# A fused layer pair of 33 pipelined steps on one core: centering split around the variances, one scatter moved ahead on GpSimd, one register load moved ahead on TensorE

## The chip, the core and the metric

The kernel runs on one core of one Trainium2 chip. The metric is the device time in microseconds (us) of one execution. Engines are named as the profile names them: PE is TensorE (PEld its weight loads, PEldq the sequencer that feeds them), DVE is VectorE, ACT is ScalarE, POOL is GpSimd, SP is SyncE (which only starts transfers here).

## The reference, cut to what matters

The input holds 128 sequences of 64 tokens with 256 features. Two layers follow each other; each picks its weights by a number that belongs to the sequence.

```python
def layer0(x, condition, ...):          # condition 0, 1, 2 per sequence
    out_nr  = gelu(x @ w1_nr  + b1_nr)  @ w2_nr  + b2_nr      # condition 0
    out_tsr = gelu(x @ w1_tsr + b1_tsr) @ w2_tsr + b2_tsr     # condition 1
    h = gelu(x @ w1_sr + b1_sr)                               # condition 2: 256 -> 512
    h = gelu(h @ w2_sr + b2_sr)                               # 512 -> 256
    out_sr = h @ w3_sr + b3_sr
    y = x + where(condition == 0, out_nr, where(condition == 1, out_tsr, out_sr))
    return layernorm(y) * gamma + beta

def layer1(x, domain_id, ...):          # 16 experts, 64 wide
    hidden = gelu(x @ down_W.T + down_b)
    hidden = hidden @ expert_W[idx].T + expert_b[idx] + domain_emb[idx]
    y = x + hidden @ up_W.T + up_b
    return layernorm(y) * ln_gamma + ln_beta
```

The whole reference computes all three branches and selects; the kernel computes only the branch that a sequence needs.

## The kernel before, in words

**Slots and steps.** The kernel sorts the sequences by condition on the chip and packs four of one kind into a slot of 256 tokens, held as two tiles of 128 tokens. Here there are 33 slots: first those of the three-layer kind (`sr`, slots 0 to 8), then those of the two-layer kinds. A software pipeline handles one slot per step. In step g, TensorE finishes the first layer of slot g (`ps_z`), transposes the normalised slot g-1 (`ps_t`), runs the adapter of slot g-2 (`ps_u`, `ps_d`) and begins slot g+1 (`ps_h`). VectorE works on the statistics of slot g and, later in the same step, on those of the second norm of slot g-2, splits the input of slot g+2 into a high and a low part, and finishes slot g-3. Fp32 products are made from three products of high and low parts, so the low parts `x_lo` (VectorE, L665) and `h_lo` (GpSimd, L482) are operands of TensorE.

**What sets the order.** The order on every engine is written by hand. Each engine runs its own loop over the steps: two steps per turn on VectorE, ScalarE, GpSimd and SyncE, four steps per turn on TensorE (L281 is the jump back). Engines wait for each other by counting semaphores, named for what is ready: `h1_lo`, `x_lo`, `rstd`, `zn_act`, `yt_act`.

**TensorE, two-layer step** (`finish_other`): the slot's kind is loaded into a register (`kind_of`), `down` makes `ps_d` (L1222), a branch picks the kind of step, `last_layer` makes `ps_z` (L1157 with the high parts, L1162 with the low ones; their addresses are worked out from the kind in registers), `start_two` makes `ps_h` (L1089), then `adapter` loads the expert's two table addresses (`tables_of`), transposes (L1179), adds residuals (L1124) and multiplies with the tables (L1209).

**TensorE, three-layer step** (`finish_sr`): kind, `down`, first half of the middle layer (L1260, L1261, and L1263 with `h_lo`), first half of the next slot's first layer (L1089, which waits for `x_lo`), second half of the middle layer (its L1263 waits for `h1_lo`), input residual (L1124), second half of the first layer, the table addresses, transposes, `last_layer`, the expert.

**VectorE** (L828 to L856): `first_stats` (`st<-ps_z`, L691), `first_moments` (`mv`, L698), `variances` (`ve`, L703), `center` (`n`, two tiles, L727), `second_stats` (`st<-ps_u`, L714), `input_low` (`x_lo`, L665), `second_moments` (L721), `minus_mean` (`nm`, L707), `finish` (`o`, L767), `add_bias` (L677), `copy_second_tables` (L743). `nm` lets ScalarE write `zn`.

**GpSimd**: in a three-layer step it makes the low part of `h2`, of the first half of `h1` (`h0_lo`), the powers `rs` of the variances (L489), the low part of the second half of `h1` (`h1_lo`), and then starts two indirect DMAs, the scatters of tile 1 (L508) and tile 0 (L515) of a slot finished a step earlier. The scatters begin with step 4. In a two-layer step the low parts are half as large, in the same order.

## Time and profile before

| | |
|---|---|
| median of 3 timed runs | 267.99 us (267.77 to 269.57) |
| time of the profiled execution | 270.54 us |
| its span, first to last instruction | 268.7 us |
| PE busy | 249.6 us (93%) |
| DVE busy | 206.6 us (77%) |
| ACT busy | 190.9 us (71%) |
| POOL busy | 174.8 us (65%) |
| mean granted TensorE clock | 0.987 |
| register loads by TensorE's sequencer (L338) | 66 |

The page gives busy times per engine and the chain of work that ended last. TensorE is nearly always busy, but the end of a matmul is modelled in this profile, so what counts is where its idle times stand and what ended them. Between about 60 and 105 us the steps are three-layer ones, 11.3 us each; from about 118 to 240 us they are two-layer ones, four of them in 23.6 us.

### The profile page before, as it was taken

How to read it: one execution, taken by the hardware profiler on the slowest of the kernel's cores; microseconds unless marked ns; L12 is line 12 of the kernel's file. 1: busy time of each engine (PE TensorE's matmuls, PEld its weight loads, DVE VectorE, ACT ScalarE, POOL GpSimd, SP SyncE). 2: the span in 40 equal slices, each digit the busy share in tenths (PEclk: the TensorE clock that was granted, in tenths of full speed). 3: DMA queues.
4: the chain of work that ended last, by engine and by line, in shares of the span. 5: the costliest groups of instructions: out<-in, count | busy, mean ns of one | idle time of the engine just before them, and what ended most of it. 6: DMA issues, size and time to landing. Idle time of an engine off the chain costs nothing.

```text
span 268.7 us, 8023 instructions
## 1 busy us (share of the span) xinstructions
PE 249.6 (93%) x2114; PEld 219.9 (82%) x2115; DVE 206.6 (77%) x717; ACT 190.9 (71%) x450; POOL 174.8 (65%) x188
## 2 busy tenths in 40 slices
PE   8998999989898898899999999999999999999960
PEld 7698898979788797799988888998888899887630
DVE  6769643472835628599989989998998999899893
ACT  3578479577494777578688877868887887878640
POOL 3134474463755857588778878887887888779451
PEclk9999999999999999999999999999999999999995
DMA  6472011011121120223323333332333333231315
GB/s 182 105 260 63 12 42 43 4 43 30 32 61 41 39 68 29 59 68 96 90 83 93 88 91 84 88 98 78 98 88 88 82 94 98 78 99 54 74 42 121
DMA packets 41640, 20.71 MB, mean 77 GB/s; under 512 B 37431, under 2 KB 39181, under 8 KB 41614
## 3 DMA queue, kind: packets, MB, share of 16 engines
q1 hardware_dynamic: 37625, 12.10, 18.7%
q0 software_dynamic: 2592, 7.08, 7.5%
q10 hardware_dynamic: 1396, 1.19, 1.7%
q8 instruction: 15, 0.25, 0.4%
q14 instruction: 12, 0.09, 0.1%
HBM read 11.69 MB, written 8.65 MB: 76 GB/s over the span
## 4 chain that ended last, share of the span: by engine, by line
PE 64%; DVE 13%; issue 9%; POOL 6%; ACT 4%; DVEq 1%; ACTq 1%; DMA 1%; POOLq 0%
PE ps_h L1089 20%; PE ps_z L1157 11%; PE ps_u L1209 6%; PE ps_z L1162 5%; PE ps_z L1124 4%; PE ps_t L1179 4%; PE ps_d L1222 4%; POOL h_lo L482 3%; PE ps_u L1124 3%; POOL rs L489 2%; DVE x_lo L665 2%; DVE st L714 2%; DVE n L727 2%; ACT yt L937 2%; ACT h L903 1%
## 5 line engine op out<-in xcount | busy, mean ns | idle before, releaser
L482 POOL TENSOR_TENSOR h_lo<-h,h_hi 128x256 fp32r<-128x256 f32 (+1 forms) x75 | 70.4, 939 | 51.3 <-ACT h L903 50.1
L910 ACT ACTIVATE zn<-ps_z,nm,rs 128x256 f32<-128x256 f32 x66 | 33.7, 561 | 30.5 <-DVE nm L707 28.9
L691 DVE BATCH_NORM_STATS2 st<-ps_z 128x6 f32<-128x256 f32 x66 | 24.8, 416 | 37.1 <-PE ps_z L1162 37.0
L489 POOL TENSOR_TENSOR rs<-ve,minus_half 128x4 f32<-128x4 f32 (+1 forms) x38 | 38.2, 1005 | 19.8 <-DVE ve L703 19.2
L903 ACT ACTIVATE h_hi<-ps_h,per_feature_sb 128x256 fp32r<-128x256 f32 x84 | 38.6, 493 | 13.9 <-PE ps_h L1089 8.9
L903 ACT ACTIVATE h<-ps_h,per_feature_sb 128x256 f32<-128x256 f32 x84 | 38.8, 499 | 0.0
L508 POOL DMA_INDIRECT out<-o,out_rows_now x27 | 34.9, 1292 | 4.8 <-issue 4.8
L937 ACT ACTIVATE yt<-ps_t,per_feature_sb 128x256 f32<-128x256 f32 x66 | 34.0, 574 | 4.2 <-PE ps_t L1179 3.4
L665 DVE TENSOR_TENSOR x_lo<-x,x_hi 128x512 fp32r<-128x512 f32 x33 | 31.2, 946 | 6.3 <-ACT x_hi L889 6.3
L1209 PE MATMUL ps_u<-tables,stack 65*64 x132 | 35.6, 392 | 0.3 <-ACT stack L921 0.3
L1209 PE MATMUL ps_u<-second_table,stack 65*64 65x256 f32 x132 | 35.6, 392 | 0.0
L1157 PE MATMUL ps_z<-last_hi,h_hi 128*128 (+1 forms) x132 | 35.5, 304 | 0.0
L1157 PE MATMUL ps_z<-last_lo,h_hi 128*128 (+1 forms) x132 | 32.1, 279 | 0.0
L515 POOL DMA_INDIRECT out<-o,out_rows_now x27 | 26.5, 980 | 8.2 <-issue 8.2
L767 DVE SCALAR_TENSOR_TENSOR o<-n,rs,per_feature_sb 128x256 f32<-128x256 f32 x64 | 28.8, 490 | 0.3
L727 DVE SCALAR_TENSOR_TENSOR n<-ps_u,mv,per_feature_sb 128x256 f32<-128x256 f32 x66 | 28.8, 477 | 0.0
L1157 PEld LDWEIGHTS ps_z<-last_hi,h_hi 128*128 128x128 f32 x132 | 24.8, 188 | 4.1 <-issue 4.1
L1089 PE MATMUL ps_h<-x_hi,w_two_hi 128*128 128x256 f32 x96 | 27.4, 285 | 0.0
L714 DVE BATCH_NORM_STATS2 st<-ps_u 128x6 f32<-128x256 f32 x66 | 25.1, 421 | 2.3 <-PE ps_u L1209 1.0
L1089 PE MATMUL ps_h<-x_hi,w_two_lo 128*128 128x256 f32 x96 | 26.8, 279 | 0.0
L1089 PE MATMUL ps_h<-x_lo,w_two_hi 128*128 128x256 f32 x96 | 26.7, 278 | 0.0
L921 ACT ACTIVATE stack<-ps_d,per_feature_sb 64x128 f32<-64x128 f32 x66 | 24.4, 369 | 1.9 <-PE ps_d L1222 0.7
(150 smaller groups left out, 649.4 us busy)
## 6 DMA issues: line engine op xcount, KB each, us to landing
x<-in_x_feat SPq DMA_DIRECT2D x130, 64.0 KB
out<-o SPq DMA_DIRECT2D x18, 64.0 KB, 2.0
out<-o,out_rows_now POOLq DMA_INDIRECT x54
last_sb<-in_last_w SPq DMA_DIRECT2D x1, 768.0 KB, 4.8
w_sr_sb<-in_w_sr SPq DMA_DIRECT2D x1, 512.0 KB, 3.9
w_sr_sb<-in_w_sr ACTq DMA_DIRECT2D x1, 512.0 KB, 4.8
w_two_sb<-in_w_two SPq DMA_DIRECT2D x1, 512.0 KB, 5.6
out<-o ACTq DMA_DIRECT2D x6, 64.0 KB, 2.4
```

Source lines behind the costliest of these rows:

```text
L482: pool.tensor_tensor(dst, full, high.bitcast(F32), ALU.subtract).then_inc(ready, 1)
L489: pool.tensor_tensor(RS[p][:, norms, :], VE[p][:, norms, :], half_of_two[:, norms, :], ALU.pow).then_inc(rstd, 1)
L508: pool.indirect_dma_start(out_rows, row, O[p][:, 1, :], None).then_inc(sc_out[p], 16)
L665: dve.tensor_tensor(XL[p][:, :, :, :], XF[p][:, :, :, :], XH[p][:, :, :, :].bitcast(F32), ALU.subtract).then_inc(x_lo, 1)
L714: dve.bn_stats(ST[1][p][:, t, :], UP[p][:, t, :]).then_inc(stat[1], 1)
L727: ins = dve.scalar_tensor_tensor(out=N2[p][:, t, :], in0=UP[p][:, t, :], scalar=MV[step][:, 1, t, 0:1], in1=G2[:, 0, :], op0=ALU.subtract, ...
L903: ins = act.activation(dst[:, m, :], src[m], ACT.Gelu, bias=COL[:, bass.ds(col + m, 1)])
L910: ins = act.activation(ZN[:, t, :], ZP[p][:, t, :], ACT.Identity, bias=NM[p][:, t:t + 1], scale=RS[p][:, 0, t:t + 1])
L937: ins = act.activation(YT[q][:, c, :], TP[:, c, :], ACT.Identity, bias=COL[:, COL_BETA1 + c:COL_BETA1 + c + 1], scale=COL[:, COL_G1 + c:CO ...
L1089: ins = pe.matmul(out_ap, lhs[a], rhs[b], start=first and n == 0, stop=last and n == 2)
L1157: pe.matmul(ZP[p][:, t, :], h2h[:, c, t * P:(t + 1) * P], rows(half, c), start=False, stop=False)
L1209: ins = pe.matmul(UP[p][own, t, :], S[p][:, t, own], table, start=False, stop=(t == TT - 1))
```

## The change: what it does

It has three parts. On VectorE, `center` is cut into its two tiles: tile 0 now stands between `first_stats` and `first_moments`, tile 1 stays behind `variances`. On GpSimd, tile 1's scatter moves ahead of the low part of h1's second half in the three-layer branch; in the two-layer branch it stays behind both low parts. On TensorE, `tables_of` moves from the middle of the step to its start, behind `kind_of` and ahead of `down`.

GpSimd, in its loop over the steps:

```diff
                 with pool.If(g + 1 < b_sr):
                     low(h1l[:, 0:2, :], h1[:, 0:2, :], h1h[:, 0:2, :], h0_full, h0_lo, g + 1)
                     powers(g, i, p, where)
+                    if where in (MAIN, LAST2):
+                        store_tile1(g - 4, p)
                     low(h1l[:, 2:4, :], h1[:, 2:4, :], h1h[:, 2:4, :], h1_full, h1_lo, g + 1)
                 with pool.Else():
...
-                store(g, where)
+                    if where in (MAIN, LAST2):
+                        store_tile1(g - 4, p)
+                if where in (MAIN, LAST2):
+                    store_tile0(g - 4, p)
```

VectorE:

```diff
+            def center_tile(slot, p, step, t):
+
                 dve.wait_ge(stat[1], 2 * TT * slot + 2 * TT)
-                for t in range(TT):
-                    ins = dve.scalar_tensor_tensor(out=N2[p][:, t, :], in0=UP[p][:, t, :],
-                                                   scalar=MV[step][:, 1, t, 0:1], in1=G2[:, 0, :],
-                                                   op0=ALU.subtract, op1=ALU.mult)
-                ins.then_inc(n2_made, 1)
+                return dve.scalar_tensor_tensor(out=N2[p][:, t, :], in0=UP[p][:, t, :],
+                                                scalar=MV[step][:, 1, t, 0:1], in1=G2[:, 0, :],
+                                                op0=ALU.subtract, op1=ALU.mult)
...
                 for slot in on_slot(g, 0, where):
                     first_stats(slot, p)
+                for slot in on_slot(g, 3, where):
+                    center_tile(slot, q, p, 0)
                 for slot in on_slot(g, 0, where):
                     first_moments(slot, p)
                 variances(p, BOTH)
                 for slot in on_slot(g, 3, where):
-                    center(slot, q, p)
+                    center_tile(slot, q, p, 1).then_inc(n2_made, 1)
```

TensorE:

```diff
-            def adapter(g, p, where):
-
-                at = [tables_of(slot) for slot in on_slot(g, 2, where)]
+            def adapter(g, p, where, at):
+
...
-                at = [tables_of(slot) for slot in on_slot(g, 2, where)]
                 pe.wait_ge(h2_full, g + 1)
...
+                at = None
                 if where != DRAIN and (where != HEAD or g >= 0):
                     kind = kind_of(pe, g)
+                    for slot in on_slot(g, 2, where):
+                        at = tables_of(slot)
                 for slot in on_slot(g, 2, MAIN if where == DRAIN else where):
                     down(slot, p, MAIN)
```

The order of GpSimd in the three-layer branch of a loop step, before (names in brackets are the semaphores it waits for):

```order
L481 REGISTER_ALU
L482 TENSOR_TENSOR h_lo<-h,h_hi 128x512 [waits h0_full]
L489 TENSOR_TENSOR rs<-ve,minus_half 128x4 [waits var]
L482 TENSOR_TENSOR h_lo<-h,h_hi 128x512 [waits h1_full]
L550 UNCONDITIONAL_BRANCH
```

and now:

```order
L481 REGISTER_ALU
L482 TENSOR_TENSOR h_lo<-h,h_hi 128x512 [waits h0_full]
L489 TENSOR_TENSOR rs<-ve,minus_half 128x4 [waits var]
L505 REGISTER_ALU
L508 DMA out<-o,out_rows_now 8960x256 [waits o1_made]
L482 TENSOR_TENSOR h_lo<-h,h_hi 128x512 [waits h1_full]
L544 UNCONDITIONAL_BRANCH
```

Tile 1's scatter stands between the powers and the second low part; before, it came behind the branch.

TensorE at the start of a step in its loop, before (`ps_d` is `down`, L1157 the first products of `last_layer`):

```order
L338 ISA
L338 TENSOR_LOAD ids
L1222 MATMUL ps_d<-yt,per_feature_sb 64x128 [waits yt_act]
L1222 MATMUL ps_d<-yt,per_feature_sb 64x128 x3
L1342 COMPARE_AND_BRANCH
L1303 REGISTER_ALU
L1157 ISA [waits h1_hi]
L1157 MATMUL ps_z<-last_hi,h_hi 128x256
```

and now (all lines behind the edits are numbered four or five higher, L1157 is L1161):

```order
L338 ISA
L338 TENSOR_LOAD ids
L338 ISA
L338 TENSOR_LOAD ids
L1226 MATMUL ps_d<-yt,per_feature_sb 64x128 [waits yt_act]
L1226 MATMUL ps_d<-yt,per_feature_sb 64x128 x3
L1347 COMPARE_AND_BRANCH
L1305 REGISTER_ALU
L1161 ISA [waits h1_hi]
L1161 MATMUL ps_z<-last_hi,h_hi 128x256
```

The second load stood between L1089 and the transposes of L1179 and is gone there.

VectorE at the start of a step in its loop, before:

```order
L691 BN_STATS st<-ps_z 128x6
L695 ISA
L698 BN_AGGR mv<-st 128x2 [waits stat1]
L698 BN_AGGR mv<-st 128x2
L699 REGISTER_ALU
L703 TENSOR_SCALAR ve<-mv 128x4 [waits stat1]
L725 REGISTER_ALU
L727 SCALAR_TENSOR_TENSOR n<-ps_u,mv,per_feature_sb 128x256 [waits stat2]
L727 SCALAR_TENSOR_TENSOR n<-ps_u,mv,per_feature_sb 128x256
L714 BN_STATS st<-ps_u 128x6 [waits u_ps]
```

and now:

```order
L690 BN_STATS st<-ps_z 128x6
L729 REGISTER_ALU
L730 SCALAR_TENSOR_TENSOR n<-ps_u,mv,per_feature_sb 128x256 [waits stat2]
L694 ISA
L697 BN_AGGR mv<-st 128x2 [waits stat1]
L697 BN_AGGR mv<-st 128x2
L698 REGISTER_ALU
L702 TENSOR_SCALAR ve<-mv 128x4 [waits stat1]
L730 SCALAR_TENSOR_TENSOR n<-ps_u,mv,per_feature_sb 128x256 [waits stat2]
L713 BN_STATS st<-ps_u 128x6 [waits u_ps]
```

One of the two centering instructions now stands ahead of the moments and of `ve`.

## Rows read from the trace of the kernel before

**Rows 1.** From the page: share of the chain that ended last, by engine

```profile
PE 64%; DVE 13%; issue 9%; POOL 6%; ACT 4%; DVEq 1%; ACTq 1%; DMA 1%; POOLq 0%
```

**Rows 2.** Timeline of TensorE, steps of three-layer slots (start us, us, line, tiles, idle before)

```profile
59.85 0.38 PE L1089 MATMUL ps_h<-x_hi,w_sr_hi 128*128 128x256 f32 x1 [0.91 <-DVE x_lo L665]
80.80 0.63 PE L1263 MATMUL ps_t<-h_lo,w_sr_hi 128*128 128x256 f32 x4
82.32 0.39 PE L1089 MATMUL ps_h<-x_hi,w_sr_hi 128*128 128x256 f32 x1 [0.89 <-DVE x_lo L665]
93.59 0.39 PE L1089 MATMUL ps_h<-x_hi,w_sr_hi 128*128 128x256 f32 x1 [0.89 <-DVE x_lo L665]
```

**Rows 3.** Timeline of VectorE in one of these steps

```profile
77.97 0.76 DVE L691 BATCH_NORM_STATS2 st<-ps_z 128x6 f32<-128x256 f32 x2 [4.96 <-PE ps_z L1162]
78.87 0.25 DVE L698 BATCH_NORM_AGGREGATE mv<-st 128x2 f32<-128x6 f32 x2
79.16 0.17 DVE L703 TENSOR_SCALAR ve<-mv 128x4 f32<-128x4 f32 x1
79.25 0.88 DVE L727 SCALAR_TENSOR_TENSOR n<-ps_u,mv,per_feature_sb 128x256 f32<-128x256 f32 x2
80.72 1.55 DVE L665 TENSOR_TENSOR x_lo<-x,x_hi 128x512 fp32r<-128x512 f32 x1
```

**Rows 4.** Timeline of GpSimd in the same step

```profile
79.41 1.04 POOL L489 TENSOR_TENSOR rs<-ve,minus_half 128x4 f32<-128x4 f32 x1 [0.83 <-DVE ve L703]
80.44 1.27 POOL L482 TENSOR_TENSOR h_lo<-h,h_hi 128x512 fp32r<-128x512 f32 x1
```

**Rows 5.** Timeline, one slot earlier than the first scatter: VectorE, then GpSimd

```profile
58.28 1.52 DVE L665 TENSOR_TENSOR x_lo<-x,x_hi 128x512 fp32r<-128x512 f32 x1
57.97 1.28 POOL L482 TENSOR_TENSOR h_lo<-h,h_hi 128x512 fp32r<-128x512 f32 x1
```

**Rows 6.** Timelines around the last three-layer step: GpSimd, then TensorE

```profile
102.97 1.28 POOL L482 TENSOR_TENSOR h_lo<-h,h_hi 128x512 fp32r<-128x512 f32 x1
104.75 0.63 PE L1263 MATMUL ps_t<-h_lo,w_sr_hi 128*128 128x256 f32 x4
106.46 0.66 PE L1124 MATMUL ps_z<-ident,x 128*128 128x128 f32 x4 [1.08 <-DVE x L677]
```

**Rows 7.** Timelines in a two-layer step: GpSimd, GpSimd, VectorE

```profile
130.42 0.72 POOL L482 TENSOR_TENSOR h_lo<-h,h_hi 128x256 fp32r<-128x256 f32 x1
131.32 1.29 POOL L508 DMA_INDIRECT out<-o,out_rows_now  x1 [0.18 <-issue]
130.92 0.77 DVE L665 TENSOR_TENSOR x_lo<-x,x_hi 128x512 fp32r<-128x512 f32 x1
```

**Rows 8.** Register loads of TensorE's sequencer (PEldq), duration ns min/median/max, start us

```profile
L338 PEldq TENSOR_LOAD <-ids x1: 309/309/309, 123.3 to 123.3; - x1
L338 PEldq TENSOR_LOAD <-ids x1: 545/545/545, 120.7 to 120.7; - x1
L1144 PEldq EVENT_SEMAPHORE  x1: 51/51/51, 121.7 to 121.7; - x1
```

**Rows 9.** Line 1157 behind a loop's jump, then in another step, same columns

```profile
L1157 PEldq ALU_OP  x1: 32/32/32, 124.7 to 124.7; - x1
L1157 PEld LDWEIGHTS ps_z<-last_hi,h_hi x1: 186/186/186, 124.8 to 124.8; 128*128 128x128 f32 x1
L1157 PEldq ALU_OP  x1: 32/32/32, 130.1 to 130.1; - x1
L1157 PEld LDWEIGHTS ps_z<-last_hi,h_hi x1: 187/187/187, 130.6 to 130.6; 128*128 128x128 f32 x1
```

**Rows 10.** The jump back of TensorE's loop from 85 us on, same columns

```profile
L281 PEldq FUSED_REGOPS  x6: 78/78/78, 89.3 to 217.5; - x6
```

**Rows 11.** Timelines: ScalarE's wait for TensorE, then TensorE's for ScalarE

```profile
134.32 0.47 ACT L903 ACTIVATE h_hi<-ps_h,per_feature_sb 128x256 fp32r<-128x256 f32 x1 [1.37 <-PE ps_h L1089]
136.13 0.66 PE L1222 MATMUL ps_d<-yt,per_feature_sb 128*64 128x128 f32 x8 [0.24 <-ACT yt L937]
```

More of the change, by code:

```diff
@@ L515, in store_tile0 @@
                 pool.indirect_dma_start(out_rows, row, O[p][:, 0, :], None).then_inc(sc_out[p], 16)
-            def store(g, where):
-                if where in (MAIN, LAST2):
-                    store_tile1(g - 4, p)
-                    store_tile0(g - 4, p)
             def scale(slot, q, p, count):
@@ L723, in center @@
             def center(slot, p, step):
+                center_tile(slot, p, step, 0)
+                center_tile(slot, p, step, 1).then_inc(n2_made, 1)
+            def center_tile(slot, p, step, t):
                 dve.wait_ge(stat[1], 2 * TT * slot + 2 * TT)
-                for t in range(TT):
-                    ins = dve.scalar_tensor_tensor(out=N2[p][:, t, :], in0=UP[p][:, t, :],
-                                                   scalar=MV[step][:, 1, t, 0:1], in1=G2[:, 0, :],
-                                                   op0=ALU.subtract, op1=ALU.mult)
-                ins.then_inc(n2_made, 1)
+                return dve.scalar_tensor_tensor(out=N2[p][:, t, :], in0=UP[p][:, t, :],
+                                                scalar=MV[step][:, 1, t, 0:1], in1=G2[:, 0, :],
+                                                op0=ALU.subtract, op1=ALU.mult)
             def last_variances(slot, p, q):
@@ L1232, in adapter @@
                 for slot in on_slot(g, 2, where):
-                    expert(slot, p, where, at[0])
+                    expert(slot, p, where, at)
             def start_sr(g, q, where, half):
@@ L1271, in middle_layer_half, with finish_sr @@
                 return middle_layer(g, half, False)
-            def finish_sr(g, p, where):
+            def finish_sr(g, p, where, at):
                 q = 1 - p
@@ L1295, in finish_sr, with finish_other @@
                 for slot in on_slot(g, 2, where):
-                    expert(slot, p, where, at[0])
-            def finish_other(g, p, where, kind):
+                    expert(slot, p, where, at)
+            def finish_other(g, p, where, kind, at):
                 for slot in on_slot(g, 0, where):
@@ L1304, in finish_other @@
                 start_two(g, 1 - p, where)
-                adapter(g, p, where)
+                adapter(g, p, where, at)
             kind = None
@@ L1342, in _ @@
                     with pe.If(g >= b_sr):
-                        finish_other(g, p, where, kind)
+                        finish_other(g, p, where, kind, at)
                     with pe.Else():
-                        finish_sr(g, p, where)
+                        finish_sr(g, p, where, at)
                 if where == HEAD and g < 0:
```

## The prediction, on record before the changed kernel ran

> **What bounds the kernel now.** I read the chain of waits first, then TensorE's timeline for what ended its idle times, then the other engines' timelines at those places. TensorE holds 64% of the chain, and VectorE and GpSimd together 19% [rows 1]. So a wait is worth something where TensorE stands still. The reader is to see two regimes. In three-layer steps TensorE stops once per step ahead of L1089, for 0.89 to 0.91 us, until `x_lo` is there [rows 2]; 59.85, 82.32 and 93.59 are shown, and the fourth such wait is at 71.06 with 0.85. In two-layer steps it hardly waits for data; there its own sequencer is the thing to look at [rows 8, 9].
>
> **Why `x_lo` is late.** In the step of rows 3 and 4, `x_lo` starts at 80.72 and takes 1.55 us, while GpSimd's second `h_lo` runs from 80.44 to 81.71 [rows 3, 4]. In a two-layer step `x_lo` takes 0.77 us, and it ends 0.55 us after GpSimd's `h_lo` ends (131.69 against 131.14), although the scatter runs from 131.32 on [rows 7]. In the three-layer step the distance is the same: 82.27 against 81.71 is 0.56. So `x_lo` stands still until GpSimd's subtraction is over, needs some 0.6 us then, and a scatter that starts after it does not hold it up. The Trainium skill, page "SBUF — State Buffer", section "SBUF: two separate sides", states the same as an exclusive lock: a VectorE operation with two SBUF inputs and a GpSimd operation that reads SBUF don't share, the one that starts first keeps the ports, the other blocks fully. The trace agrees on the blocking (0.55 and 0.56 us behind GpSimd's end). [...]
>
> **Part 1, the scatter ahead of the second `h_lo`** (four steps, g = 4 to 7). `rs` ends at 80.45 [rows 4]; the scatter takes 1.29 us and starts 0.18 after what is ahead of it [rows 7], so `h_lo` starts at about 80.45 + 0.18 + 1.29 = 81.9 and not 80.44. `x_lo` then has the ports to itself and is ready at about 80.7 + 0.65 = 81.35. TensorE's L1263 group starts at 80.80 and ends at 81.43 as modelled [rows 2], so the wait goes. That is 0.85 + 0.89 + 0.89 = 2.6 us for the waits at 71.06, 82.32 and 93.59. The delayed `h_lo` ends at about 83.2 plus what part 2 adds, 0.2; TensorE would ask for it 2.5 us after L1089 begins (two groups of matmuls later), at about 83.9. It is covered by 0.5 us. In the last three-layer step no first layer lies between the two halves: TensorE asks at 104.75, the `h_lo` of 102.97 to 104.25 will end 1.67 later, at 105.9, and TensorE waits 1.2 us [rows 6]. Today it waits 1.08 us right behind it for the input's bias, which `x_lo` would have brought forward [rows 6]; the one wait takes the place of the other, and I charge 0.2 us. The second scatter is no longer behind the first without a break, but nobody waits for it.
>
> **Part 2, centering.** It removes and adds no instruction. `mv` starts at 78.87, 0.14 after the statistics end [rows 3]; one tile of `n` is half of 0.88, and fills that gap. So `ve` comes 0.44 - 0.14 = 0.3 later at most, and 0.2 if the tile overlaps its neighbours as the two tiles overlap; I take 0.2. `x_lo` starts 0.14 to 0.2 earlier. In the step before the first scatter this changes who comes first: `x_lo` starts at 58.28 and `h_lo` at 57.97 [rows 5]; now `x_lo` at about 58.1 and `h_lo`, which follows `rs` and so `ve`, at 57.97 + 0.2 = 58.17. If VectorE is first, the wait of 0.91 at 59.85 goes too; if not, it grows by 0.2. I take the gain, as the likelier by some 0.07 us. In two-layer steps `x_lo` ends 0.55 behind GpSimd's `h_lo` [rows 7], which follows `ve` where `rs` waits for it; nothing is gained there, and `zn` can come 0.2 later. I charge nothing for that: TensorE reaches its transposes behind twelve matmuls of L1089, and if this cover is gone a step pays up to 0.2. At the drain the powers stand on the chain and the last ordinary step pays 0.2.
>
> **Part 3, the register load.** TensorE's sequencer loads the kind in 0.309 us and the two table addresses in 0.545 [rows 8]. Where the second load stands now, the matmuls of L1089 cover it, and behind it the sequencer waits for `zn` anyway (the wait of L1144 at 121.7, 0.4 after the load ended at 121.3) [rows 8]; its removal there gives TensorE nothing. At the start of a step the sequencer works out the addresses of L1157 after the load. Behind the loop's jump it finishes at 124.7, and the first weights go at 124.8: no slack. In another step it finishes at 130.1 and they go at 130.6: 0.4 of slack [rows 9]. A second load of 0.545, with its address operation, is some 0.55 us more. It is paid in full behind the jump, and mostly covered elsewhere, since a late step leaves `zn` early for the next one. The loop jumps back six times from 89 us on, once among the three-layer steps [rows 10]: 5 x 0.55 = 2.75 us. At the sixth, `down` would be some 0.35 late and takes that from what the wait at 93.59 gives back. Bounds: 0 if the load can be overlapped; 22 two-layer steps x 0.545 = 12 us if no slack counted; the row at 124.7 is the nearest, hence 2.75.
>
> **The sum.** -0.91 - 2.63 + 0.2 + 0.35 = -3.0 for the three-layer steps, + 2.75 for the two-layer ones, + 0.2 at the drain: -0.05 us on the profiled time of 270.54 (span 268.7), which is 2.55 above the median of 267.99. The steps are the same in both, so I subtract from the median: 267.9 us, no change. A measurement of this kernel can tell about 1%, or 2.7 us, from no change.
>
> **Rivals.**
> 1. *Faster: the load isn't paid.* If the second load comes while the sequencer is held anyway (at 136.13 `down` waits for `yt` [rows 11]), or costs 0.1, the three-layer gain stands alone: 267.99 - 3.0 + 0.2 = 265.2. Connected with it: ScalarE gets TensorE's signal 1.37 us late once in four steps [rows 11], in a step in which the loads of several sequencers fall together; if moving TensorE's load ends this, each of five is worth 0.24 (TensorE's own wait) to 1.37, so 1.2 to 6.9 us more. With the middle of the lower half of it, some 2, and the load unpaid, 263.5. For: in a step such as that of rows 11 the sequencer has idle time in plenty. Against: rows 9 leave no slack. Chance 0.30 in all.
> 2. *Slower: every two-layer step pays.* The slack of 0.4 in an ordinary step is smaller than 0.55. If `zn` is not early enough for the sequencer to catch up, each of the 17 steps that are not behind a jump pays 0.15 to 0.2. That is 3 us: 267.9 + 3.0 = 270.9, slower by 1.1%. The point from which it decides is 0.4 us of added sequencer time in a step whose `zn` is not earlier than now. Chance 0.13.
> 3. *Slower: the scatter holds the ports.* By the mechanism of rows 7 a GpSimd operation that is first blocks `x_lo`. If the scatter were first in the three-layer steps (it starts at about 80.8, `x_lo` at 80.55) and blocked as a subtraction does, `x_lo` would end at 80.8 + 1.29 + 0.55 = 82.6, and the waits would grow by 0.35 and not shrink: 267.9 + 2.6 + 1.0 = 271.5. [...] Against: rows 7 show a scatter beside `x_lo` with no delay. Chance 0.07.
> 4. *The forecast*, gains and costs that cancel: 0.50, with 266.3 to 269.8 as its own range (the race for the ports is 1.1 us, each load may be 0.1 us off, which is 0.5).
>
> **How the numbers follow.** Faster by over 1% (below 265.3): most of rival 1 and the lower edge of the forecast, 0.29. Slower by over 1% (above 270.7): rivals 2 and 3 and a little of the forecast, 0.18. Within 1%: 0.53. The range that leaves out no more than 2 in 10 runs from 264.2, inside rival 1, to 270.9, the time of rival 2.
>
> **What would show it.** The waits for `x_lo` ahead of L1089 at some 70, 81 and 91 us should be under 0.2 us, `x_lo` near 0.7 us there; one new wait for `h_lo` of about 1 us in the last three-layer step. The load of the tables should stand 0.1 behind that of the kind, and L1157 should begin 0.5 us later after `down` only behind the jump, making four two-layer steps 24.1 us and not 23.6. If they still take 23.6, part 3 is wrong and rival 1 holds; if `x_lo` still takes 1.5 us, part 1 is wrong.

## The result and the profile after

The changed kernel takes 270.49 us (median of 11 runs, 269.17 to 272.02), the kernel before 268.96 us (11 runs, 267.54 to 271.26). The ratio is 1.0072, 95% interval [1.0045, 1.0098]: slower by 0.7%, where I forecast 267.9 us and no change. The time lies in the forecast's range, but the likeliest case was not what happened.

The two profiled executions show nothing of it: both have a span of 268.7 us (270.53 us after, 270.54 before), at a clock of 0.988 and 0.987. So the first question is what the profile of before stood for; the second, where the parts went.

**Three-layer steps.** VectorE, then GpSimd, of the changed kernel, in the step that answers to [rows 3, 4]:

```profile
77.78 0.48 DVE L730 SCALAR_TENSOR_TENSOR n<-ps_u,mv,per_feature_sb 128x256 f32<-128x256 f32 x1
78.85 0.68 DVE L664 TENSOR_TENSOR x_lo<-x,x_hi 128x512 fp32r<-128x512 f32 x1
79.60 0.13 DVE L706 SCALAR_TENSOR_TENSOR nm<-mv,rs 128x2 f32<-128x2 f32 x1
79.71 2.75 DVE L769 SCALAR_TENSOR_TENSOR o<-n,rs,per_feature_sb 128x256 f32<-128x256 f32 x2
82.38 0.34 DVE L676 TENSOR_SCALAR x<-x,slot_bias 128x256 f32<-128x256 f32 x1
```

```profile
77.95 1.04 POOL L489 TENSOR_TENSOR rs<-ve,minus_half 128x4 f32<-128x4 f32 x1 [1.62 <-DVE ve L702]
79.20 1.24 POOL L508 DMA_INDIRECT out<-o,out_rows_now  x1 [0.20 <-issue]
80.47 1.30 POOL L482 TENSOR_TENSOR h_lo<-h,h_hi 128x512 fp32r<-128x512 f32 x1
```

`x_lo` takes 0.68 us and not 1.55, as forecast, and TensorE no longer waits for it. But the two tiles of `o` take 2.75 us where they took 0.87: the first alone takes 2.35 us and not 0.47, and ends only 0.3 us behind the second `h_lo`, which is over at 81.77. The bias of the input behind them (L676) is late, and TensorE waits for that:

```profile
83.07 0.66 PE L1128 MATMUL ps_z<-ident,x 128*128 128x128 f32 x4 [0.40 <-DVE x L676]
```

The waits of TensorE's matmuls, summed over the changed kernel (line waited for: us in total, times, longest), have lost "DVE x_lo", 3.5 us in 4 waits before. Of the rows below the first stood at 1.1 us in one wait before, and the third is new:

```profile
PE ps_z L1128 <- DVE x L676: 1.8, 4, 0.5
PE ps_d L1226 <- ACT yt L941: 1.1, 5, 0.3
PE ps_t L1266 <- POOL h_lo L482: 1.0, 1, 1.0
```

**Two-layer steps.** The two loads now stand together behind the jump (TensorE's sequencer, duration ns min/median/max, first and last start us):

```profile
L338 PEldq TENSOR_LOAD <-ids x2: 308/426/543, 145.5 to 146.0; - x2
```

and `down` comes late six times:

```profile
PEld ps_d L1226 <- issue: 2.9, 6, 0.6
```

The wait of ScalarE of [rows 11] is there once in each turn of the loop (four steps), in the profile of before as in that of after (here the second of five in the changed kernel). I call a wait of 1.3 us and more for `ps_h` a late signal:

```profile
156.76 0.47 ACT L907 ACTIVATE h_hi<-ps_h,per_feature_sb 128x256 fp32r<-128x256 f32 x1 [1.42 <-PE ps_h L1093]
```

**A table of all profiles.** From TensorE's timelines: T1 is the start of the first last layer (L1157 before, L1161 after) behind the three-layer steps, T2 that of the one 21 steps later. "Late" counts the late signals from 117 us on.

```
kernel                           T1      T2 - T1   late   time us   ratio to before
before, first profile            119.08  123.99    5      270.54    (this execution)
before, profiled again (e9)      119.06  121.66    1      268.20    (this execution)
after                            117.33  125.75    5      270.49    1.0072
e1  load only                    119.14  123.49    3      269.99    1.0052
e2  scatter + split centering    117.39  122.57    1      267.57    0.9975
e3  scatter only                 117.48  121.50    1      266.69    0.9963
e4  split centering only         114.79  122.57    1      264.86    0.9866
e5  split + load                 114.98  126.25    5      268.74    1.0020
e6  x_lo issued earlier          114.61  135.95    0      279.42    1.0420
e7  e2, bias ahead of o          115.07  128.43    0      271.14    1.0111
e8  e5 once more                 115.84  126.49    5      268.98    1.0020
e10 e5, four loads at the top    120.14  134.93    8      282.91    1.0562
e11 e5, tile 0 not stored        115.93  121.57    0      264.13    0.9859
e12 e4, tile 0 not stored        114.81  121.61    0      264.13    0.9867
e13 after, tile 0 not stored     117.18  121.61    0      266.19    0.9935
e14 e5, second scatter later     115.77  132.90    0      277.28    1.0360
e15 split in three-layer only    114.78  121.43    1      263.46    0.9837
```

The rest of the document reads this table. The scatter and the centering show mostly in T1, the load in T2 - T1. T1 also holds the start of the kernel: the first last layer of all stands at 53.7 us in most profiles, but 0.8 to 0.9 us later in e8 and e11, 0.4 in e14 and e15, and 1.7 in e10.

### The profile page after: what moved, and what is told of

Its sections match the earlier page's. It is cut to its first block, busy times and chain, and to the rows that moved or that the text cites. A ratio compares the mean times of both kernels' runs of the same rounds, so it can differ in the third digit from the quotient of the medians.

```text
span 268.7 us, 8050 instructions
## 1 busy us (share of the span) xinstructions
PE 251.2 (93%) x2114; PEld 219.9 (82%) x2115; DVE 209.4 (78%) x717; ACT 192.1 (71%) x450; POOL 175.5 (65%) x188
## 4 chain that ended last, share of the span: by engine, by line
PE 64%; issue 11%; DVE 11%; POOL 6%; ACT 4%; DVEq 2%; ACTq 0%; POOLq 0%
PE ps_h L1093 18%; PE ps_z L1161 11%; PE ps_u L1213 7%; PE ps_z L1166 5%; PE ps_z L1128 4%; PE ps_d L1226 4%; PE ps_t L1183 4%; POOL h_lo L482 3%; PE ps_u L1128 3%; POOL rs L489 2%; DVE o L769 2%; DVE st L713 2%; PE ps_t L1038 2%; ACT yt L941 2%; DVE st L690 1%
## 5 line engine op out<-in xcount | busy, mean ns | idle before, releaser
L482 POOL TENSOR_TENSOR h_lo<-h,h_hi 128x256 fp32r<-128x256 f32 (+1 forms) x75 | 71.4, 953 | 47.5 <-ACT h L907 46.0
L489 POOL TENSOR_TENSOR rs<-ve,minus_half 128x4 f32<-128x4 f32 (+1 forms) x38 | 38.2, 1006 | 23.5 <-DVE ve L702 23.2
L769 DVE SCALAR_TENSOR_TENSOR o<-n,rs,per_feature_sb 128x256 f32<-128x256 f32 x64 | 36.5, 609 | 0.3
L1161 PE MATMUL ps_z<-last_hi,h_hi 128*128 (+1 forms) x132 | 35.5, 304 | 0.0
L664 DVE TENSOR_TENSOR x_lo<-x,x_hi 128x512 fp32r<-128x512 f32 x33 | 28.5, 863 | 6.0 <-ACT x_hi L893 6.0
L1161 PE MATMUL ps_z<-last_lo,h_hi 128*128 (+1 forms) x132 | 32.2, 279 | 0.0
L730 DVE SCALAR_TENSOR_TENSOR n<-ps_u,mv,per_feature_sb 128x256 f32<-128x256 f32 x66 | 30.6, 470 | 0.0
L1161 PEld LDWEIGHTS ps_z<-last_hi,h_hi 128*128 128x128 f32 x132 | 24.8, 188 | 4.1 <-issue 4.1
```

Source lines behind the costliest of these rows:

```text
L482: pool.tensor_tensor(dst, full, high.bitcast(F32), ALU.subtract).then_inc(ready, 1)
L489: pool.tensor_tensor(RS[p][:, norms, :], VE[p][:, norms, :], half_of_two[:, norms, :], ALU.pow).then_inc(rstd, 1)
L730: return dve.scalar_tensor_tensor(out=N2[p][:, t, :], in0=UP[p][:, t, :], scalar=MV[step][:, 1, t, 0:1], in1=G2[:, 0, :], op0=ALU.subtract ...
L769: dve.scalar_tensor_tensor(out=O[o][:, t, :], in0=N2[q][:, t, :], scalar=RS[p][:, 1, t:t + 1], in1=G2[:, 1, :], op0=ALU.mult, op1=ALU.add) ...
L1161: pe.matmul(ZP[p][:, t, :], h2h[:, c, t * P:(t + 1) * P], rows(half, c), start=False, stop=False)
```

## The experiments

**e9: the kernel before, unchanged, once more.**

> The kernel before, unchanged, profiled once more: how much of its first profile is one outcome among several. Theory J (the kernel before has executions with a late signal of TensorE in each turn of the loop and executions without): this one shows between 0 and 4 waits of ScalarE of over 1.3 us for `ps_h` in the two-layer steps and not 5, and a span shorter by 0.4 to 0.5 us for each that is missing (264.5 to 268.3 us). Rival K (they belong to this order of instructions): again five, and a span within 0.4 us of 268.7.

One wait of over 1.3 us (168.97, 1.44), a span of 266.4 us, 268.2 us in all. T1 is the same to 0.02 us, T2 - T1 is 2.33 us shorter: 0.58 us for each of four late signals. So theory J holds, with 0.58 and not 0.4 to 0.5 us for each. The wait, ScalarE of e9:

```profile
168.97 0.47 ACT L903 ACTIVATE h_hi<-ps_h,per_feature_sb 128x256 fp32r<-128x256 f32 x1 [1.44 <-PE ps_h L1089]
```

The profile that the prediction was made from was one of the longer outcomes of this kernel: that explains most of the 1.6 to 2.6 us by which it stood above the medians, and why two profiles of one span can belong to kernels 0.7% apart.

**e1: the register load alone.** Part 3's lines of the diff on the kernel before.

```diff
                     kind = kind_of(pe, g)
+                    for slot in on_slot(g, 2, where):
+                        at = tables_of(slot)
```

> Only part 3: TensorE loads the two table addresses with the kind, ahead of `down`; scatter and centering stay as before. Theory A (the load behind the loop's jump is paid on TensorE's path): 5 two-layer jumps x 0.4 to 0.55 us and one three-layer jump x 0.35, so +2.0 to +3.1 us, a ratio of 1.008 to 1.012, with about six waits put down to issue ahead of `down` (L1226 of the kernel after), 0.4 to 0.5 us each. Rival B (the loss of the whole comes from the split centering, whose `ve` is later in the two-layer steps): ratio 1.000, within 0.002. Rival C (every two-layer step pays 0.15 to 0.2 us beside the jumps): +5 us, ratio 1.02.

1.0052 [1.0018, 1.0086], +1.4 us. Seven waits of `down` for issue, 3.0 us in all, as theory A says, but only +1.83 in T2 - T1 against e9, with three late signals and not one. A price below A's. The turns of the loop without a late signal tell the two apart: they take 23.27 and 23.22 us here (119.14 to 142.41, 213.64 to 236.86), and 22.99 and 22.96 in e9 (119.06 to 142.05, 188.81 to 211.77); the step of the jump takes 6.00 and 5.95, and in e9 5.71 and 5.69. So on the kernel before, the load itself costs some 0.3 us behind the jump in these two turns, about half of the 0.55 of the prediction.

**e2: scatter and split centering, without the load.** `at = [tables_of(slot) ...]` stands again where it stood before, in `adapter` and `finish_sr`.

> Parts 1 and 2 without part 3: the addresses are loaded where the kernel before loads them. Theory A: what the three-layer steps gained in the profile (1.75 us up to the first two-layer step, with a jump of 0.35 in it) stands alone, -1.8 to -2.1 us, a ratio of 0.992 to 0.994, and the waits ahead of `down` put down to issue are gone. Rival B (the split centering costs 0.1 to 0.2 us in each of 22 two-layer steps): a ratio of 1.000 to 1.008, with two-layer steps still longer than in the kernel before.

0.9975 [0.9945, 1.0006]; 2.9 us below the changed kernel by the medians, 2.6 by the two ratios. That is what the load costs this kernel; four late signals come with it.

**e3: the scatter alone.** GpSimd's lines of the diff on the kernel before.

```diff
                     powers(g, i, p, where)
+                    if where in (MAIN, LAST2):
+                        store_tile1(g - 4, p)
                     low(h1l[:, 2:4, :], h1[:, 2:4, :], h1h[:, 2:4, :], h1_full, h1_lo, g + 1)
```

> Part 1 alone: tile 1's scatter ahead of the second `h_lo` on GpSimd; centering and load as before. Theory A: the waits for `x_lo` at three of the four places go (0.85, 0.89, 0.89), but `o` on VectorE, which reads two SBUF operands, is now held for about 1.9 us by the scatter and the `h_lo` behind it, and the bias of the input comes 0.4 to 0.5 us too late for TensorE in each of them: -2.63 + 4 x 0.45 = -0.8 us, ratio 0.997; the wait of 0.91 for `x_lo` at 59.85 stays. Rival D (a scatter does not hold `o`; the late `o` is an effect of the split centering): `o` stays near 0.87 us for both tiles, and the gain is 2.4 us, ratio 0.991.

0.9963 [0.9931, 0.9996]. The time is theory A's, the reason only half. Here it is `nm` that is held and not `o`. VectorE, then GpSimd, of e3:

```profile
80.04 0.68 DVE L664 TENSOR_TENSOR x_lo<-x,x_hi 128x512 fp32r<-128x512 f32 x1
80.78 1.59 DVE L706 SCALAR_TENSOR_TENSOR nm<-mv,rs 128x2 f32<-128x2 f32 x1
82.37 0.87 DVE L766 SCALAR_TENSOR_TENSOR o<-n,rs,per_feature_sb 128x256 f32<-128x256 f32 x2
```

```profile
79.97 1.04 POOL L508 DMA_INDIRECT out<-o,out_rows_now  x1 [0.20 <-issue]
81.04 1.31 POOL L482 TENSOR_TENSOR h_lo<-h,h_hi 128x512 fp32r<-128x512 f32 x1
```

`nm` (0.12 us when free) begins 0.26 us ahead of `h_lo` and still ends with it, at 82.37. It was held from 80.78 on, while of GpSimd's operations only the scatter ran.

**e4: the split centering alone.** VectorE's lines of the diff on the kernel before.

```diff
+                for slot in on_slot(g, 3, where):
+                    center_tile(slot, q, p, 0)
                 for slot in on_slot(g, 0, where):
                     first_moments(slot, p)
                 variances(p, BOTH)
                 for slot in on_slot(g, 3, where):
-                    center(slot, q, p)
+                    center_tile(slot, q, p, 1).then_inc(n2_made, 1)
```

> Part 2 alone: centering divided around the variances. Theory A: the race for the ports at the step without a scatter goes to VectorE (-0.9 us); the other three-layer steps keep their wait for `x_lo`, perhaps shorter by 0.1; two-layer steps cost nothing or 0.1 us each: between -0.9 and +1.3 us, ratio 0.997 to 1.005. Rival B (the split is what made the whole slower): +2 to +4 us, ratio 1.008 to 1.015, two-layer steps longer by 0.1 to 0.2 us each, with the statistics or `rs` later by as much.

0.9866 [0.9818, 0.9913], 264.86 us: far outside what both theories gave. T1 is 4.3 us earlier. VectorE, then GpSimd, of e4:

```profile
78.26 0.68 DVE L665 TENSOR_TENSOR x_lo<-x,x_hi 128x512 fp32r<-128x512 f32 x1
79.01 1.10 DVE L707 SCALAR_TENSOR_TENSOR nm<-mv,rs 128x2 f32<-128x2 f32 x1
80.10 0.87 DVE L770 SCALAR_TENSOR_TENSOR o<-n,rs,per_feature_sb 128x256 f32<-128x256 f32 x2
```

```profile
78.40 1.69 POOL L482 TENSOR_TENSOR h_lo<-h,h_hi 128x512 fp32r<-128x512 f32 x1
```

The split wins the race in every three-layer step, not in one: `x_lo` begins 0.14 us ahead of `h_lo` where it began 0.28 behind [rows 3, 4], a shift of 0.42. GpSimd's subtraction is held instead (1.69), and `nm` is held until that is over at 80.1, but nothing longer; the scatter comes later and `o` runs beside it in 0.87. Steps take 10.1 us, against 11.26 before and 10.67 with the scatter ahead. So the scatter, which I priced at -2.6 us, costs 2.7 us once the centering is split (e2 against e4: 267.57 and 264.86; T1 117.39 and 114.79).

**e6: another way to win the race.** On the kernel before:

```diff
                 for slot in on_slot(g, -2, where):
                     input_low(slot, p)
+                for slot in on_slot(g, 2, where):
+                    second_stats(slot, p)
```

(and `second_stats` gone from ahead of it).

> The kernel before, with one edit only: `x_lo` is issued on VectorE ahead of the statistics of `ps_u` and not behind them, so it starts some 0.7 us earlier; centering is not split. Theory F (the gain of the split centering is that VectorE's `x_lo` comes ahead of GpSimd's second `h_lo`): `x_lo` takes 0.7 us, the waits for it ahead of TensorE's first layer go, three-layer steps take 10.1 to 10.3 us and not 11.26, the time is 264.5 to 266 us, ratio 0.984 to 0.990. Rival G (the gain comes from something else in the split, the tile of `n` that is done early or the later `ve`): the steps stay above 10.6 us and the ratio above 0.993.

T1 is 114.61: steps of 10.1 us are there without any split, so theory F holds for the mechanism. The time is 279.42 us, 1.042 [1.0385, 1.0454], far above F's range, since two-layer steps now take 6.2 to 6.8 us: VectorE stands waiting for `x_hi`, and the statistics behind it are late. Theory F had left that out.

```profile
147.78 0.82 DVE L665 TENSOR_TENSOR x_lo<-x,x_hi 128x512 fp32r<-128x512 f32 x1 [0.85 <-ACT x_hi L889]
148.53 0.75 DVE L714 BATCH_NORM_STATS2 st<-ps_u 128x6 f32<-128x256 f32 x2
```

**e7: the bias ahead of `o`.** On e2:

```diff
+                for slot in on_slot(g, -2, where):
+                    dve.wait_ge(x_lo, slot + 1)
+                    add_bias(slot, p)
                 for slot in on_slot(g, 3, where):
                     finish(slot, i - 2 if p == 0 else i - 1, q, where)
```

(and `add_bias` gone from behind it).

> Parts 1 and 2 without part 3 (267.57 us), with one further edit: VectorE adds the input's bias ahead of the two tiles of `o`, not behind them. Theory H (what part 1 costs is that `o` stands still from the middle of the scatter to the end of the second `h_lo`, and delays the bias TensorE waits for): the waits of 0.4 to 0.5 us for `x` go and three-layer steps fall from 10.66 to 10.1 to 10.3 us, 265.0 to 266.2 us. Rival I (the cost of part 1 is the second `h_lo` itself, which comes later for the middle layer, or the bias is held up as `o` is): steps stay at 10.5 to 10.7 us and the time within 0.7 us of 267.6.

The waits for `x` are gone, T1 is 115.07 and the steps take 10.1 us, as theory H says. But the bias itself is now what stands still, as rival I had it:

```profile
79.12 2.60 DVE L676 TENSOR_SCALAR x<-x,slot_bias 128x256 f32<-128x256 f32 x2
81.65 0.15 DVE L767 COPY out_rows_now<-out_rows 128x2 int32 x1
81.72 0.87 DVE L769 SCALAR_TENSOR_TENSOR o<-n,rs,per_feature_sb 128x256 f32<-128x256 f32 x2
```

It ends at 81.7 and not at 83.0, which is enough for TensorE. In two-layer steps the new order costs 5.9 us in T2 - T1 (most steps take 6.0 to 6.3 us), and the kernel takes 271.14 us, 1.0111 [1.0076, 1.0145], outside both theories' ranges. The cause of that cost stays open.

**e5, e8: the load on the split centering.** Part 3's lines on e4; e8 with a second `tables_of(slot)` ahead of the first.

> The split centering together with the moved register load, without the moved scatter. The split alone ran at 264.86 us, its four two-layer steps at 23.2 us with no signal of TensorE's later than 1.3 us in them after the first. Theory A (the load is paid in TensorE's sequencer behind the loop's jump, 0.35 to 0.5 us at each of six jumps): +2.1 to +3.0 us, 267.0 to 267.9 us, and 23.6 to 23.7 us for every four two-layer steps also where ScalarE gets no late signal. Rival E (the load costs 0.2 us per jump or less, and the rest is that `h_hi` on ScalarE waits 1.3 to 1.6 us for TensorE's `ps_h` more often): +0.5 to +1.2 us where such waits stay at one, +0.45 more for each further one, and 23.3 to 23.4 us for four steps without one.

> The split centering and the moved load, with the load of the two addresses issued twice at the top of each step of TensorE (the first one's values unused): twice the suspected cost. Theory A (no slack behind the jump, 0.4 us in an ordinary step): another 0.55 us behind each of six jumps and 0.1 to 0.2 in each of the 17 other two-layer steps: +5 to +7 us over the kernel with one load. Rival E (most of a load is covered also behind the jump): less than +2.5 us over it.

268.74 and 268.98 us, both 1.0020 ([0.9998, 1.0041] and [0.9997, 1.0044]). e8's unused load was dropped in compiling, so it is a second run of e5 and its expectation was not put to a test. The load costs 3.9 us here, more than either theory said. Of it, 0.3 us lie in the one three-layer step behind a jump (84.1 to 94.5: 10.41 us, 10.13 in e4). Four two-layer steps take 24.0 us, each turn with one late signal of 1.40 to 1.62 us. Without the load they take 23.2, with a late signal only in the first two-layer step.

**e11, e12: the same pair without the second scatter.** In both, GpSimd doesn't store tile 0 (the count that waits for scatters is halved to match):

```diff
-                row = bass.IndirectOffsetOnAxis(ap=OUT_NOW[p][:, 0:1], axis=0)
-                pool.indirect_dma_start(out_rows, row, O[p][:, 0, :], None).then_inc(sc_out[p], 16)
```

> The split centering and the moved load; GpSimd does not store tile 0 (its scatter, the second of a step, is left out). Theory M (TensorE's signals are held when a group of first-layer matmuls ends beside the second scatter, which the later `down` brings about): no wait of ScalarE over 1.3 us for `ps_h` in the two-layer steps, four of them at 23.6 us and not 24.0, 1.8 to 2.2 us less than with the second scatter, 266.5 to 267 us. Rival N (the late signals have nothing to do with the scatter): again four or five of them, four steps at 24.0 us, 268.2 to 268.8 us.

> The split centering alone, with tile 0 not stored (the second scatter of a step is left out): the pair to the kernel with the load moved and the same left out. With both theories 264.0 to 264.9 us, four two-layer steps at 23.2 us or less, since no signal was late in the kernel with both scatters after its first two-layer step. The difference of the pair is then the load's own price: 0.4 us at each of six jumps, 2.0 to 2.8 us, under theory A; under 1 us if the sequencer's time is covered.

Both 264.13 us (0.9859 and 0.9867, each within 0.0027): the pair shows no difference. No signal is late. `down` still waits for the sequencer eight times, 3.4 us in all:

```profile
PEld ps_d L1225 <- issue: 3.4, 8, 0.5
```

and the step of the jump takes 6.02 us (138.90 to 144.92), but the four up to 162.11 take 23.21, as in e12: the steps behind it take 5.7 us where e12's take 5.8, so TensorE makes up for it. So theory A falls for the kernels with the split centering: in their two-layer steps the load itself costs nothing that can be seen, and nearly all of its 3.9 us in e5 go by way of the late signals. The one three-layer step behind a jump does pay (10.39 us against 10.12), and on the kernel before, where free steps average 5.74 us (e9), e1's jumps pay 0.3. Theory M holds, and more strongly than I had put it (264.1 and not 266.5). One reservation: leaving out the scatter also frees GpSimd for some 1.3 us in each step, and no run takes away the late signals alone.

**e13: the changed kernel without the second scatter.**

> The changed kernel with tile 0 not stored (the second scatter of a step is left out). Theory M (the moved load costs only through TensorE's signals that are held beside the second scatter): no wait of ScalarE over 1.3 us for `ps_h` in the two-layer steps, four of them at 23.2 us; the changed kernel's 270.5 us less five turns of the loop x 0.8 us, 266.2 to 267.0 us. Rival A (the load is paid by TensorE's sequencer, 0.4 us at each of six jumps, in the changed kernel): 268.5 to 269.5 us.

266.19 us, 0.9935 [0.9910, 0.9960], no late signal, T2 - T1 121.61. Leaving the scatter out brings e4 0.7 us, and the changed kernel 4.3. The remaining 3.6 are what the load costs by way of the late signals, by these medians; e2 gives 2.9. A turn of the loop with a late signal is 0.8 us longer here (24.0 against 23.2 us).

**e10: a truly longer top of the step.** On e5, both halves of the last layer take their own load of the kind, and each tile its own load of the addresses:

```diff
-                    kind = kind_of(pe, g)
+                    kind = (kind_of(pe, g), kind_of(pe, g))
-                        at = tables_of(slot)
+                        at = [tables_of(slot)[0], tables_of(slot)[1]]
```

> The split centering and the moved load, with the step's top made longer for TensorE's sequencer: the kind and the addresses come in four loads of one value (0.31 us each, and what goes with them) and not in one of one value and one of two (0.31 + 0.545), some 0.4 to 0.5 us more in each step. (The kernel that was to load twice had lost its unused load in compiling: its trace counts 68 loads by TensorE, as the one with one load does, so it was a second run of that kernel.) Theory A (what the sequencer does at the top is paid behind the loop's jump): another 0.4 to 0.5 at each of six jumps, and 0 to 0.2 in each of 17 other two-layer steps, +2.4 to +6 us over 268.74. Rival L (once TensorE is behind the scatters, the size of the load doesn't matter): within 1 us of 268.7.

The trace counts 132 loads by TensorE and not 68: a step loads twice 0.31 and twice 0.54 us, so some 0.9 us were added and not 0.4 to 0.5. 282.91 us, 1.0562 [1.0531, 1.0594]. `down` waits for its sequencer ("issue") in 19 steps:

```profile
PEld ps_d L1228 <- issue: 19.1, 19, 1.5
```

T2 - T1 grows by 8.7 us over e5, 0.41 in each of 21 steps. Eight signals are late and not five, so a part of it goes by way of them. Rival L falls. The first 0.55 us at the top were covered (e11), the next 0.9 cost less than a half of their length. That is the mechanism of the prediction's rival 2, beyond a point that the change had not reached.

**e14: the second scatter later.** On e5, GpSimd fills an unused tile ahead of it and waits for that to be done.

```diff
+                pool.memset(idle[:, :], 0.0).then_inc(idle_made, 1)
+                pool.wait_ge(idle_made, slot + 1)
```

> The split centering and the moved load (268.74 us), nothing left out; GpSimd fills an unused tile of 128x256 ahead of the second scatter, so that it starts an estimated 0.3 to 0.6 us later. Theory M with the moment deciding (a signal is held where the group of matmuls ends when the second scatter has begun or is about to; the groups ended from 0.09 before... after its start to 0.19 us ahead of it): all groups now end 0.3 us or more ahead of it, no wait over 1.3 us in the two-layer steps, four of them at 23.2 to 23.3 us, 264.6 to 265.6 us. Rival O (the scatter's descriptors are the cause wherever it stands, or GpSimd's added work is paid): late signals again, or steps over 5.9 us, and 268.5 us or more.

277.28 us, 1.0360 [1.0316, 1.0405]. No wait of 1.3 us, as theory M says (every group ends 1.06 us or more ahead of the scatter), but the edit was too large to decide what that is worth: GpSimd, of e14,

```profile
150.26 0.33 POOL L514 MEMSET idle<- 128x256 f32 x1
151.43 0.96 POOL L519 DMA_INDIRECT out<-o,out_rows_now  x1 [0.84 <-POOL idle L514]
```

starts the second scatter 1.18 us behind the end of the first, where e5 starts it 0.30 behind, and `h_lo` is late for TensorE's weight loads (8.5 us in 22 waits; 2.9 in 4 in e5). Whether a small delay would save the load is open.

**e15: split only where a three-layer step follows.** On e4, `with dve.If(g + 1 < b_sr):` around the split order and `dve.Else()` around the old one.

> Centering is split only in steps that are followed by a three-layer step, by a branch on VectorE; in the others both tiles of `n` stand behind the variances as in the kernel before; scatter and load as in the kernel before. Theory P (the split costs 0.02 to 0.03 us in each two-layer step and gains only in three-layer ones): three-layer steps at 10.1 us, the whole from 264.2 to 264.9 us. Rival Q (the branch, or signals of TensorE held more often in the rhythm of the old order, cost more than that): 265.2 to 266.5 us, with one or more additional waits of over 1.3 us for `ps_h`.

263.46 us, 0.9837 [0.9808, 0.9865], below theory P's range; T2 - T1 is 121.43, 1.14 less than in e4. T1 is as in e4 though all began 0.4 us later: the step into T1, which now has the old order, takes 6.84 us and not 7.16. It is the fastest of all kernels here, 2.3% below the changed kernel by the two ratios. Both profiles have one late signal, so the split costs 0.05 us in each of 21 two-layer steps, and the branch nothing that can be seen.

## Why the prediction was wrong

Against the kernel before as e9 shows it, the changed one gains 1.7 us up to T1 and loses 4.1 from T1 to T2. I had -3.0 (with the jump in it) and +2.75, so both terms were off, in the same direction. That the sum of -0.05 us met the two profiled times to 0.04 us was luck: between those two profiles, T1 moved by -1.75 and T2 - T1 by +1.76 us. The 0.2 us at the drain didn't come: from T2 to the end of the span it is 25.6 us in both. The step that failed worst is the first.

**Part 1, failed.** "That is 0.85 + 0.89 + 0.89 = 2.6 us for the waits", priced against the kernel before, though part 2 stood beside it. The waits did go. On the kernel before, part 1 alone even pays, though less than that: T1 is 1.6 us earlier and the ratio 0.9963 (e3). But part 2 alone takes the waits away too (e4), and what part 1 adds is its cost: `o` is held from the middle of the scatter to the end of the `h_lo` behind it, the bias is late, and TensorE waits 0.4 to 0.5 us four times. In e2 against e4 part 1 costs 2.7 us; with the bias ahead of `o` the steps are back at 10.1 us (e7). I had looked for operations with two SBUF inputs at one place only, `x_lo`, and not asked what stands behind it on VectorE when GpSimd's `h_lo` is moved there. The one new wait for `h_lo` in the last three-layer step came as forecast (1.0 us).

**Part 2, right in kind, too small.** I counted the race in the step of [rows 5] and took the gain, -0.91; that step shrank from 11.28 to 10.09 us. But in the steps of [rows 3, 4] the same working gives it too: `x_lo` was 0.28 us behind, and I had `x_lo` 0.14 to 0.2 earlier and `h_lo` 0.2 later. That is 0.34 to 0.4, enough. I didn't apply it, since part 1 had already moved that `h_lo` away. Alone it is worth 4.3 us of T1 and 3.8 in time. For two-layer steps I charged nothing; it is 0.05 us each (e4 against e15), about 1 us in all, and 0.3 in the last three-layer step.

**Part 3, the size near, the mechanism wrong.** +2.75 forecast, +2.9 measured (after against e2); that the two are near is luck. The prediction has it as 5 x 0.55 of sequencer time. The six waits of `down` for issue are there, but e11 against e12 shows them to cost nothing in two-layer steps where no signal is late. On the kernel before, the mechanism is real and half as large, 0.3 us behind a jump (e1). The cost is rival 1's link with its sign turned: moving the load didn't end ScalarE's late waits, it made them come in every turn (5 against 1 in e2).

**The base, failed silently.** The profiled execution stood 2.55 us above the median, and I subtracted it as a constant. Most of it was four late signals of 0.58 us (2.3 us), and they sat where part 3 acts. The profile of the changed kernel stands 0.04 us above its own median, so nothing of that distance carried over. From a profile with one late signal I would have read [rows 11] as a cost that could come, and not as one that could go.

**The rivals.** Rival 1: the load is unpaid in itself in two-layer steps (e11, e12), but not in this kernel; a late signal, for which it allowed 0.24 to 1.37 us, is worth 0.58 (e9) to 0.8 us (e13). Rival 2, every step pays: not here, it begins with the next 0.9 us (e10). Rival 3, the scatter holds the ports: I set it at 0.07, and it has half of what happened. The scatter doesn't hold `x_lo`, which runs beside it in 0.68 us (e3); but where a subtraction follows close behind it, VectorE is held from about the scatter's middle on. The Trainium skill, page "SBUF — State Buffer", section "SBUF: two separate sides", sets a VectorE operation with two SBUF inputs only against a GpSimd operation that reads SBUF. The traces agree for subtractions (`x_lo` 1.55 us beside one, 0.68 without), but not for the powers, which read SBUF too and hold nothing (in e6 `x_lo` begins at 77.74, 0.39 us before powers end at 78.13, and takes 0.68 us); whether a scatter counts as such an operation it doesn't say, and what the traces show of it is in the section on the hardware below.

## What to carry to other kernels

Price the parts of a change against each other and not each against the old kernel: a part whose gain another part already brings leaves only its costs, here 2.7 us. When an engine's operation is moved to win a race for ports, list everything with the same needs that will then stand beside it, and not only the operation that was late. And before subtracting from a profile, ask how much of its distance from the median is one mechanism that sometimes happens; profile the same kernel twice if a term of the sum lies there.

## What was not expected of the hardware

**A scatter and what is queued behind it.** In the kernel before, `o` starts 0.55 to 0.58 us into a scatter and runs in 0.87 us for both tiles, in every step but the last, at the drain; behind that scatter stands another. In the changed kernel it starts 0.51 us into a scatter (79.71 against 79.20) and is held for 1.9 us; behind that scatter stands a subtraction, 0.03 us after its end. In e3 `nm`, 0.81 us in, is held in the same way. So it looks as if the subtraction behind a scatter claims the ports some 0.3 to 0.8 us before its own span begins.

What stands close behind the scatter decides it, not the scatter. In e14 a fill of a tile, which reads nothing, follows 0.01 us behind, and `o` is free. VectorE, then GpSimd, of e14:

```profile
117.63 0.87 DVE L774 SCALAR_TENSOR_TENSOR o<-n,rs,per_feature_sb 128x256 f32<-128x256 f32 x2
```

```profile
117.06 1.29 POOL L510 DMA_INDIRECT out<-o,out_rows_now  x1 [0.18 <-issue]
118.35 0.33 POOL L514 MEMSET idle<- 128x256 f32 x1
```

In two-layer steps of e11 and e12 a subtraction comes next, but 1.4 to 1.7 us after the scatter's end, and `o`, 0.57 us into the scatter, takes 0.47 us a tile. At the drain powers follow 0.02 us behind a scatter (the changed kernel, 245.97 to 246.98), and the bias beside it takes its usual 0.61 us. All 20 operations of VectorE that are held from within a scatter (in the changed kernel, e2, e3, e7 and e13) have the subtraction 0.03 to 0.04 us behind it. The scatter's length tells nothing: it is 1.04 to 1.43 us with these. Why the claim comes ahead of the subtraction's span stays open. The bias, an operation with one SBUF tensor, is held too (e7: 2.27 us for the first tile, 2.60 for both). And the powers `rs` hold nobody, though they read SBUF: in 133 of 134 cases in all profiles, an `x_lo` or a tile of `o` that begins 0.1 us or more before they end takes its 0.67 to 0.69 or 0.47 to 0.48 us.

**Late signals.** The first half of the first layer is six matmuls; here the last of them, the second scatter and ScalarE's step, in the changed kernel, where it is held:

```profile
155.08 0.28 PE L1093 MATMUL ps_h<-x_hi,w_two_lo 128*128 128x256 f32 x1
155.30 0.96 POOL L515 DMA_INDIRECT out<-o,out_rows_now  x1 [0.30 <-issue]
```

and in e4, where it isn't:

```profile
152.28 0.28 PE L1094 MATMUL ps_h<-x_hi,w_two_lo 128*128 128x256 f32 x1
152.75 0.96 POOL L515 DMA_INDIRECT out<-o,out_rows_now  x1 [0.30 <-issue]
153.19 0.48 ACT L908 ACTIVATE h_hi<-ps_h,per_feature_sb 128x256 fp32r<-128x256 f32 x1 [0.40 <-issue]
```

In the first the group ends (155.36) 0.06 us after the scatter's start, and ScalarE begins 1.40 us after that end; in the second it ends 0.19 us before the start (152.56), and ScalarE begins 0.63 after it. Without the second scatter no signal is late in three kernels (e11 to e13). But in the changed kernel the step before the held one has the scatter at 149.50, the sixth matmul from 149.32, and ScalarE's step at 149.74, with no delay.

Counted over all profiles that have the second scatter, from 114 us on, there are 36 late signals (for two of them, in e10, the profile names another releaser). In every one the group ends, by the profile's modelled ends, at most 0.15 us before that scatter starts or while it runs (up to 0.78 us into it, in e10). Of 163 groups that end earlier than that, none has one. And in all 36 ScalarE begins 0.43 to 0.75 us after the second scatter is over (0.50 above, 156.26 to 156.76). So it looks as if the signal were held until that scatter is done. Beside the scatter isn't sufficient: more groups end there without a late signal than with one. What holds some and not the others stays open.

**A wait for the engine's own signal.** In e14 the second scatter waits for GpSimd's own fill of 0.33 us and starts 0.84 us after its end; behind another scatter it starts after 0.30. Here a delay made this way was 0.88 us long in all, two to three times the work put in.
